# A two-layer decoder on one core: value projections of the first attention moved into its loop, scores on two sets of PSUM banks, one store for four heads

## What is computed

```python
qkv = x @ w_qkv                                     # (B, L, 3, H, D), H = 16, D = 64
q, k = rope(q), rope(k);  scores = q @ k.T / sqrt(D)
kerple = -p * log1p(a * |j - i|)
combined = concat([scores over the heads, kerple over the heads])     # 32 numbers
refined = gelu(combined @ w1 + b1) @ w2 + b2                          # 16 numbers
scores = where(causal, scores + kerple + refined, -inf)
out = (softmax(scores) @ v) @ w_o
```

## Time and profile before

| | |
|---|---|
| time, median of 3 runs | 4125.24 us (4124.12 to 4130.19) |
| profiled execution: its time, its span | 4128.32 us, 4126.5 us |
| TensorE busy, share of the span | 3815.9 us, 92% |
| VectorE, ScalarE busy | 2427.9 us (59%), 1740.2 us (42%) |
| mean granted clock of TensorE | 0.984 of 2.4 GHz |
| first pass, start of stage A to first `up` | 55.71 to 125.99 us |
| starts of stage A in the four passes | 55.71, 1076.93, 2094.19, 3111.20 us |

### The profile page before, as it was taken

The page is one execution under the profiler, slowest core; times in us unless marked ns, Lnnn a source line. Parts: engine busy times, 40 slices in busy tenths (PEclk is TensorE's granted clock), DMA queues, the critical chain, the costliest instruction groups (busy, mean ns, idle before and its releaser), DMA issues.

```text
span 4126.5 us, 59377 instructions
## 1 busy us (share of the span) xinstructions
PE 3815.9 (92%) x22610; PEld 1837.7 (45%) x22610; DVE 2427.9 (59%) x6081; ACT 1740.2 (42%) x3188; POOL 152.0 (4%) x168
## 2 busy tenths in 40 slices
PE   4899899999989989999998998999999999899999
PEld 2353444345435244435543524443553443444355
DVE  5568576832466856673236676766323776676542
ACT  1655434521274643362127464336113836433511
POOL 1000020000000002000000001100000000200000
PEclk9999999999999999999999999999999999999999
DMA  5313002122331200203242210120325121012031
GB/s 174 122 43 63 19 18 54 22 96 73 102 109 43 55 19 25 57 12 104 72 127 93 43 38 18 45 48 1 115 62 162 63 51 26 19 45 48 1 126 55
DMA packets 135286, 254.49 MB, mean 62 GB/s; under 512 B 23332, under 2 KB 82724, under 8 KB 130084
## 3 DMA queue, kind: packets, MB, share of 16 engines
q1 hardware_dynamic: 134984, 250.50, 21.7%
HBM read 156.04 MB, written 44.04 MB: 48 GB/s over the span
## 4 chain that ended last, share of the span: by engine, by line
PE 74%; DVE 16%; ACT 7%; issue 2%; PEldq 0%; SPq 0%; DMA 0%; PEld 0%; DVEq 0%; POOLq 0%; ACTq 0%
PE ps L1232 11%; PE ps L588 7%; PE ps L571 6%; PE ps L1250 5%; DVE mx L754 4%; PE ps L411 4%; PE ps L515 4%; PE ps L1604 3%; PE ps L1520 3%; PE ps L576 3%; ACT a_X L1682 2%; PE ps L467 2%; PE ps L1544 2%; DVE ps L751 2%; PE ps L1563 2%
## 5 line engine op out<-in xcount | busy, mean ns | idle before, releaser
L692 ACT ACTIVATE PT<-ps 128x512 f32<-128x512 f32 (+2 forms) x1280 | 644.2, 564 | 325.2 <-PE ps L576 174.7
L1232 PE MATMUL ps<-xnT,f_w 128*128 128x512 f32 x1088 | 493.8, 598 | 0.0
L754 DVE TENSOR_REDUCE mx<-ps 128x1 f32<-128x512 f32 (+3 forms) x768 | 431.1, 618 | 76.4 <-PE ps L515 39.6
L571 PE MATMUL ps<-QS,KS 99*128 99x512 bf16 (+2 forms) x1280 | 419.1, 369 | 8.5 <-ACT PT L692 8.0
L515 PE MATMUL ps<-KS,QS 96*128 96x512 bf16 (+3 forms) x1280 | 392.2, 368 | 17.4 <-DVE mx L754 6.9
L751 DVE CUSTOM_DVE_ANT_0 ps<-ps,mneg 128x512 f32<-128x512 f32 x512 | 340.8, 718 | 82.0 <-PE ps L515 78.9
L1338 DVE TENSOR_TENSOR f_tm<-f_si,ps 128x512 f32<-128x512 f32 x128 | 88.1, 688 | 492.1 <-ACT f_si L1290 492.0
L588 PE MATMUL ps<-PT,VP 128*32 128x512 f32 (+3 forms) x2560 | 372.0, 573 | 0.0
L411 PE MATMUL ps<-mneg,identb 128*128 128x512 bf16 x1192 | 312.9, 389 | 28.5 <-DVE a_fin L1716 10.5
L1290 ACT ACTIVATE f_si<-ps 128x512 f32<-128x512 f32 x136 | 80.8, 597 | 595.5 <-PE ps L1245 576.4
L1232 PEld LDWEIGHTS ps<-xnT,f_w 128*128 128x128 f32 x1088 | 208.6, 193 | 206.5 <-issue 199.9
(11 more groups left out here) (278 smaller groups left out, 5524.1 us busy)
## 6 DMA issues: line engine op xcount, KB each, us to landing
f_w<-in_wF SPq DMA_DIRECT2D x136, 384.0 KB, 3.1
scores<-a_fin SPq DMA_DIRECT2D x64, 256.0 KB, 3.0
a_fin<-scores SPq DMA_DIRECT2D x32, 512.0 KB, 4.5
a_Y<-in_wA SPq DMA_DIRECT2D x5, 3072.0 KB, 15.1
KS<-KP SPq DMA_DIRECT2D x240, 64.0 KB, 2.3
scores<-a_fin SPq DMA_DIRECT2D x64, 192.0 KB, 2.9
a_fin<-scores SPq DMA_DIRECT2D x12, 1024.0 KB, 7.6
a_fin<-scores SPq DMA_DIRECT2D x16, 768.0 KB, 4.3
```

Of the source, the lines that this page charges most:

```text
L571: last = nc.tensor.matmul(o, m["KS"][0:KST, h, j * P:(j + 1) * P], m["QS"][0:KST, h, q0:S], start=True, stop=plain)
L692: nc.scalar.activation(m["PT"][:, mp % 2, j % 2, e, 0:w], ps[:, SLOTS + n % TURNED, 0:w], ACT.Exp, scale=HD ** -0.5).then_inc(g("exp"), 1)
L754: nc.vector.tensor_reduce(m["mx"][:, h % 2, i, f // BANK:f // BANK + 1], ps[:, k % SLOTS, 0:w], AX.X, ALU.max, negate=True).then_inc(g("sl ...
L1232: last = nc.tensor.matmul(ps[:, 2 * v + e % 2, :], m["w"][:, e % NRING, (2 * v + k) * P:(2 * v + k + 1) * P], xnT[:, k, :], start=(k == 0) ...
```

## The change

Three edits, all in stage A. The value projections leave the opening: their weights are no longer part of the big early load but get a DMA of their own into `ctxT`, a buffer that is free until chunk data need it, at the start of the stage (`v_in`); the eight products stand in the bank list of the loop, two each at k = 3, 5, 7 and 9 ahead of that k's turns, and VectorE instead of ScalarE copies them to `a_V`; the `keep_warm` of the gaps 4, 6, 8 and 10 goes. From step 10 on every second step of scores uses banks 4 to 7 (`score_base`). And a tile's four heads are stored by one DMA: the scratch tensor is laid out so that the four lie side by side for a store, and a chunk's rows apart for a load.

```diff
-            sp.dma_start(M1["w"][:, :, :], io["wA"].rearrange("(k p) c -> p k c", p=P)).then_inc(signal, 16)
+            sp.dma_start(M1["w"], io["wA"].rearrange("(k p) c -> p k c", p=P)[:, :, 0:2 * AH * AW]).then_inc(signal, 16)
...
-        sk = [nc.dram_tensor(f"scores{i}", (AU * AH, AQ * (i + 1) * P), F32, kind="Internal").ap() for i in range(NI)]
+        sk = [nc.dram_tensor(f"scores{i}", (AQ, AU * AH, (i + 1) * P), F32, kind="Internal").ap() for i in range(NI)]
...
+        V_AT = {3: (0, 1), 5: (2, 3), 7: (4, 5), 9: (6, 7)}
...
+            for u, parts in V_AT.items():
+                after[u] = [("v", e, 0) for e in parts] + after[u]
...
-        EXP_GAPS = [LAST[c] + 1 for c in range(1, SMALL)]
+        EXP_GAPS = [LAST[c] + 1 for c in range(1, SMALL) if LAST[c] not in V_AT]
...
+        def score_base(n):
+
+            return 4 if n >= 10 and n % 2 == 0 else 0
...
-                rows = sk[i].rearrange("(u h) (q j) -> h q u j", u=AU, q=AQ)
-                for hh in range(4):
-                    sp.dma_start(rows[4 * hq + hh], M2["Ss"][i][:, hh * L:(hh + 1) * L]).then_inc(g(f"out{i}"), 16)
+                rows = sk[i].rearrange("q (u h) j -> (q u) (h j)", u=AU)
+                sp.dma_start(rows[:, 4 * hq * L:4 * (hq + 1) * L], M2["Ss"][i]).then_inc(g(f"out{i}"), 16)
...
             def load(c):
                 i, r, R, L = chunk(c)
+                rows = sk[i].rearrange("q p j -> p q j")
+                place = fin(c)[:, 0:R * L].rearrange("p (q j) -> p q j", q=R)
...
-                    sp.dma_start(fin(c)[:, 0:R * L], sk[i][:, r * L:(r + R) * L]).then_inc(g(loaded(c)), 16)
+                    sp.dma_start(place, rows[:, r:r + R, :]).then_inc(g(loaded(c)), 16)
+
+            sp.dma_start(ctxT[:, :, :], io["wA"].rearrange("(k p) c -> p k c", p=P)[:, :, AC:AC + AH * AW]).then_inc(g("v_in"), 16)
...
-            def values(e):
-                if e < 4:
-                    pe.wait_ge(g("rope"), 7 + e // 2)
-                else:
-                    pe.wait_ge(g("v_up"), e - 3)
+            def values(y, e):
+                if e == 0:
+                    pe.wait_ge(g("v_in"), 16)
...
+                n = NI * hq + k
+                before = [x for x in range(n) if score_base(x) == score_base(n)]
+                if before:
+                    pe.wait_ge(g("s_up"), before[-1] + 1)
...
-                    if hq >= 2:
-                        e = NI * (hq - 2) + k
-                        act.wait_ge(g("v_mm"), e + 1)
-                        nc.scalar.activation(m["V"][:, e // 2, (e % 2) * BANK:(e % 2 + 1) * BANK], ps[:, 4 + e % 4, :], ACT.Copy).then_inc(g("v_up"), 1)
...
+                    elif what == "v":
+                        nc.vector.tensor_copy(m["V"][:, a // 2, (a % 2) * BANK:(a % 2 + 1) * BANK], bank).then_inc(g("bank_up"), 1)
```

More of the change, by code:

```diff
@@ L1369, in decoder @@
         WARM_EXP, WARM_LOAD = 9, 14
-        sk = [nc.dram_tensor(f"scores{i}", (AU * AH, AQ * (i + 1) * P), F32, kind="Internal").ap() for i in range(NI)]
-        named("A", "rope", "qk_mm", "qk_up", "s_mm", "s_up", "v_mm", "v_up", "out0", "out1", "out2", "out3", "fin0", "fin1", "fin2", "fin3", "fin_half", *(f"fin{c}" for c in range(8, 14)),
+        sk = [nc.dram_tensor(f"scores{i}", (AQ, AU * AH, (i + 1) * P), F32, kind="Internal").ap() for i in range(NI)]
+        named("A", "rope", "qk_mm", "qk_up", "s_mm", "s_up", "v_in", "out0", "out1", "out2", "out3", "fin0", "fin1", "fin2", "fin3", "fin_half", *(f"fin{c}" for c in range(8, 14)),
               "w1", "gelu", "w2", "mixed", "negm", "exp", "prob", "bank_mm", "bank_up")
         KT_A = AH * AW // P
-        AC = 3 * AH * AW
+        AC = 2 * AH * AW
         TRI_L = [(i + 1) * P for i in range(NI)]
@@ L1470, in store @@
                 sp.wait_ge(g("s_up"), NI * hq + k + 1)
-                rows = sk[i].rearrange("(u h) (q j) -> h q u j", u=AU, q=AQ)
-                for hh in range(4):
-                    sp.dma_start(rows[4 * hq + hh], M2["Ss"][i][:, hh * L:(hh + 1) * L]).then_inc(g(f"out{i}"), 16)
+                rows = sk[i].rearrange("q (u h) j -> (q u) (h j)", u=AU)
+                sp.dma_start(rows[:, 4 * hq * L:4 * (hq + 1) * L], M2["Ss"][i]).then_inc(g(f"out{i}"), 16)
             def stored(i):
-                sp.wait_ge(g(f"out{i}"), 16 * AH)
+                sp.wait_ge(g(f"out{i}"), 16 * NI)
             def load(c):
                 i, r, R, L = chunk(c)
+                rows = sk[i].rearrange("q p j -> p q j")
+                place = fin(c)[:, 0:R * L].rearrange("p (q j) -> p q j", q=R)
                 if c == 0:
-                    sp.dma_start(fin(c)[:, 0:R * L // 2], sk[i][:, r * L:r * L + R * L // 2]).then_inc(g(loaded(c)), 16)
-                    sp.dma_start(fin(c)[:, R * L // 2:R * L], sk[i][:, r * L + R * L // 2:(r + R) * L]).then_inc(g("fin_half"), 16)
-                else:
-                    sp.dma_start(fin(c)[:, 0:R * L], sk[i][:, r * L:(r + R) * L]).then_inc(g(loaded(c)), 16)
+                    sp.dma_start(place[:, 0:R // 2, :], rows[:, r:r + R // 2, :]).then_inc(g(loaded(c)), 16)
+                    sp.dma_start(place[:, R // 2:R, :], rows[:, r + R // 2:r + R, :]).then_inc(g("fin_half"), 16)
+                else:
+                    sp.dma_start(place, rows[:, r:r + R, :]).then_inc(g(loaded(c)), 16)
+            sp.dma_start(ctxT[:, :, :], io["wA"].rearrange("(k p) c -> p k c", p=P)[:, :, AC:AC + AH * AW]).then_inc(g("v_in"), 16)
             for hq in range(NI - 1):
@@ L1522, in project @@
                 last.then_inc(g("qk_mm"), 1)
-            def values(e):
-                if e < 4:
-                    pe.wait_ge(g("rope"), 7 + e // 2)
-                else:
-                    pe.wait_ge(g("v_up"), e - 3)
+            def values(y, e):
+                if e == 0:
+                    pe.wait_ge(g("v_in"), 16)
                 i, f = divmod(e, 2)
                 for k in range(KD):
-                    last = nc.tensor.matmul(ps[:, 4 + e % 4, :], xnTA[:, k, i * P:(i + 1) * P],
-                                            m["w"][:, k, 2 * HW + f * BANK:2 * HW + (f + 1) * BANK], start=(k == 0), stop=(k == KD - 1))
-                last.then_inc(g("v_mm"), 1)
+                    last = nc.tensor.matmul(ps[:, A_TURN + y % 2, :], xnTA[:, k, i * P:(i + 1) * P], ctxT[:, k, f * BANK:(f + 1) * BANK],
+                                            start=(k == 0), stop=(k == KD - 1))
+                last.then_inc(g("bank_mm"), 1)
             def scores(hq, k):
@@ L1543, in scores @@
                         r = 32 * hh
-                        last = nc.tensor.matmul(ps[:, hh, 0:(i + 1) * P], m["qk"][r:r + 32, 4 * hq + hf, i * P:(i + 1) * P],
+                        last = nc.tensor.matmul(ps[:, score_base(n) + hh, 0:(i + 1) * P], m["qk"][r:r + 32, 4 * hq + hf, i * P:(i + 1) * P],
                                                 m["qk"][r:r + 32, 4 * hq + 2 + hf, 0:(i + 1) * P], start=(hf == 0), stop=(hf == 1),
@@ L1619, in a_pe @@
                         project(8 + NI * hq + k)
[L1620 to L1622 removed]
+            pe.wait_ge(g("s_up"), 4 * NI - 1)
             keep_warm(WARM_LOAD, bank=A_DOWN)
@@ L1644, in a_pe @@
                         turn(y, a, b)
+                    elif what == "v":
+                        values(y, a)
                     elif what == "values":
```

10 lines of the change are left out of this document (5 added, 5 removed).

## The result

The changed kernel takes 4163.6 us (median of 4 runs, 4154.3 to 4166.8), the kernel before beside it 4124.7. The ratio is 1.0088 with a 95% interval of 1.0068 to 1.0108: slower by 0.9%. The forecast was 4134 with a range of 4117 to 4146; the direction was the one forecast, the size was not.

A forecast was written before the change was run, and what follows sets the result against it. TensorE bounds the kernel, at 74% of the chain and full in the opening. Opening against gaps gives +0.25 us a pass, the clock +1.9: +2.1 a pass, +8.6 in four, so 4134 on the median; range 4117 to 4146.

The forecast's parts named there:

- The opening: Stage A up to `up(0)`: products leave, scores' copies come earlier, store and load follow; gains 7.5 us a pass, bounds 6.0 to 8.5.
- The clock there: Under `up(0)`, after a 3.7 us pause of TensorE: lower clock in every pass, 2.3 a pass, net +1.9.
- The turns behind VectorE's copy at k = 5 and 7: Loop gaps: turns wait for value-product copies behind VectorE's division, delaying `up(7)` and `up(9)`; +2.0 us each.
- k = 3 is free: Loop gap ahead of `up(5)`: both value products end before ScalarE releases `up(5)`; cost 0.
- the load waits: `load(4)` to `load(6)`, issued later, hold `up(8)`, `up(10)`, `up(12)`: +0.4, +1.25, +1.6 us a pass; bounds together 2.3 to 6.0.
- the rival of the slow loads: Loop: each of the three loads takes 5.6 us, adding 3.0 a pass, total 4146; chance 11%.
- the step at k = 9: Loop, to `up(11)`: late turns show less since ScalarE already held that unit by 1.35; +1.4 us a pass.
- k = 12: Loop, ahead of `up(13)`: idle matmuls stay and 0.93 us of waiting can absorb lateness; -0.9 a pass.
- theory: Opening's gain is real, given back by turns behind a division, later loads turning from hidden to seen, and the clock.
- That the clock holds in the opening: Rival at `up(0)`: clock holds or costs what it did; +0.25 a pass, less up to 0.4; 4125 to 4126; 27%.
- That the transfers close the pause: Rival ahead of `up(0)`: store and load take 7.2 together, pause 1.7, no clock term; 4117, faster; 14%.
- Rival C: Experiments' rival, opening and loop: the clock is the main cost of the change; no chance given.

The follow-up runs named there:

- 56 short idle matmuls: The changed kernel with its 14 idle matmuls of 512 columns ahead of `up(0)` replaced by 56 of 128 columns; 4147.0 us, ratio 1.0050.
- the run with 28 idle matmuls: The changed kernel with 28 idle matmuls instead of 14 ahead of `up(0)`; 4144.1 us, ratio 1.0049.

## Why the forecast fell short

**Right.** The opening (-7.5 forecast, -8.4 measured): store and load took 3.9 + 4.6 in place of 5.0 + 4.2. The clock there (+1.9, measured +2.0). The turns behind VectorE's copy at k = 5 and 7 (+2.0 each, measured 2.0 and 2.1). That k = 3 is free. That `up(10)` and `up(12)` wait for a DMA in every pass; `up(8)` does in two of the four. In the opening two misses of the forecast partly cancel: the store was 1.1 quicker than its 5.0, the load 0.4 slower than its 4.2.

**The step that failed** is the size of the load waits, with what hangs on it. The prediction took 4.5 for `load(4)` and `load(5)`, and 0.35 more for `load(6)`, "In the trace `load(6)` alone takes 5.6, in every pass about that". The row was read as a property of `load(6)`. It belonged to a place in TensorE's program: the packet of 16 KB of instructions that was fetched during it. In the kernels with the new layout `load(6)` takes 4.3 to 4.4 in the 12 cases where no packet begins in it, and 5.1 to 6.1 in the 27 where one begins 0.6 to 3.5 us behind its issue. The change moved program and loads against each other, and the packet fell into all three, at 0.8 to 2.9 us after their issue in every pass. They took 4.8 to 6.2, and their terms came to 1.1 + 2.5 + 2.45 = 6.1 where the forecast had 3.25. (Its upper bound is written as 6.0; worked out by its own rules from loads of 5.6 it is 6.2. And 0.3 of the 1.1 is no load wait but the low clock on unit 7 in two passes.)

That is the rival of the slow loads, at 11% and 4146. The time is 18 above even that; 7 of it is the place of the two profiled executions among their runs, and the 32.0 between these is 11 above the rival's 20.6. The rival left out what a longer wait does next. At the waits of 2.37 and 2.23 the clock was low for a stretch of 3.41 each in the first pass. The loops of the four passes have nine such stretches, seven at such waits and two on unit 7: the step at k = 9 became +2.7 instead of +1.4, and k = 12 absorbed 0.1 instead of 0.9, because `up(12)`'s followers ran at 0.50. That is 2.1 a pass. A long wait makes the low stretch likely, not certain: over the fourteen kernels it stood at 25 of the 38 waits of over 2 us ahead of `up(8)`, `up(10)` or `up(12)`, and at none of the 26 between 1.0 and 1.5. With the packet moved out of the loads (56 short idle matmuls) the four steps from `up(9)` to `up(13)` are +1.45, +1.3, +1.2, -1.0, against a forecast of +1.25, +1.4, +1.6, -0.9: from `up(9)` on theory and sizes hold once the fetch is taken away.

The Trainium skill's "TensorE: Matmul & The Clock Gate" (section "Why this matters for your kernels") advises against pauses between bursts of matmuls. The trace agrees in the opening (a pause of 3.11, and 10.24 us at 0.50 that begin in it), and the run with 28 idle matmuls had 2.2 back in these steps, though its `up(0)` came 1.7 later. The Trainium skill's "DMA: Bandwidth & Descriptors" (section "Anatomy of one DMA — SWDGE (gpsimd) path") has a fit, made for the DMAs of GpSimd, by which the store of 1024 KB would take an estimated 4.4. SyncE's store here took 3.8. So on this term the page was nearer than the forecast's 5.0.

**Rivals.** That the clock holds in the opening is refuted by the row of `up(0)`. That the transfers close the pause needed `load(0)` to land before 117; it landed at 118.57, or 117.7 without the 0.87 by which this pass starts later. Rival C has part of the truth: the clock costs about 2.0 in the opening and about 2.1 in the loop, over half of the sum of a pass. In the loop it goes with the load waits: with 56 short idle matmuls the low stretches at `up(10)` to `up(12)` are gone in all four passes.

**Open.** Why a given long wait is or is not met by a low stretch, and why one falls on unit 7, was not tried. Stage A behind `up(13)` (0.7 of it behind `up(21)`) and the other stages cost 0.8 and 0.55 a pass in the changed kernel; the same code of the other stages took from -0.3 to +2.8 a pass against before in the experiments. The low stretches there differ in number and length from run to run, and what sets them was not tried either.

## What to carry to other kernels

A move of work into idle time has two tests: does it fit, and does what stands behind it (here turns, and the loads that they release) start as early as before. With three products ahead of `up(0)` and one a gap behind the turns, in place of the idle matmuls and in a bank that is free then, the move was worth 0.65%, where two a gap ahead of the turns cost 0.9%. One a gap ahead of the turns, its copy ahead of the division, did about as well (4104.7 beside 4100.9, the intervals overlap), so the place behind the turns is not shown to be the better one. When one transfer of a kind is longer than its like in every pass, look at which packets lie beside it before pricing it as its own; and ask of a longer wait what the clock does at its end.

## What the runs showed of the hardware

In the twelve profiled kernels with the new layout, 768 KB loads in which no instruction packet began took 4.3 to 4.9 (64 loads, median 4.5); with one that began 0.6 to 3.5 us after the issue 4.6 to 6.2 (66 loads, median 5.65). So a packet of 16 KB that takes 0.9 to 1.8 itself goes with a load that is 1.2 longer. Earlier and later packets did less: with one in the first 0.6 us the median is 4.7 (21 loads), with one after 3.5 us 4.5 (41 loads, four of them 5.8 to 6.35). In the old layout the two medians are 4.3 and 5.6 (11 and 14 loads), so packets of 1.5 KB instead of 6 KB cost 0.2. Fourteen more matmuls in TensorE's program moved the packet by 0.2 to 0.7 us against `load(4)` (median 0.6), in the two kernels that have them.

SyncE issued twenty stores of one head in a row at 0.65 us each, and a store of four heads takes its queue 0.3 to 1.4 (median 0.3), so four small stores hold the queue that one large one leaves free.
